# Scaling expert rows at the PSUM eviction and adding them into the output by an accumulating scatter

## The chip, the cores and the metric

The kernel runs on one core of a Trainium2 chip. The metric is the device time of one execution in microseconds (us). Engines are named as in the profile: PE is TensorE, PEld its weight loads, DVE VectorE, ACT ScalarE, POOL GpSimd, SP SyncE.

## What is computed

The program is two decoder layers on x of 8 x 256 tokens (T = 2048) and 512 features: cross-attention, a dense feed-forward layer, cross-attention again, and a mixture of 16 experts. Each is preceded by a layernorm and added to the residual. The change concerns the last of the four:

```
logits = x @ gate_w.T ; p = sigmoid(logits) ; p = p / sum(p)
w, idx = top_k(p, 2) ; w = w / sum(w)
combine = sum(one_hot(idx) * w)                     # (T, 16)
gate, up = split(x @ gate_up_proj[e])               # 512 -> 2*256, for each expert e
y[e] = (silu(gate) * up) @ down_proj[e]             # 256 -> 512
x = x + sum_e combine[:, e] * y[e]
```

## The kernel before

All of it is written by hand: every engine has its own instruction list in each stage, and semaphores order them. The stages before the experts (`load_stage`, `layernorm_stage`, `attention_stage`, `ffn_stage`) keep the residual in SBUF as `k.x_sb`, 16 tiles of 128 tokens by 512 features. The last `layernorm_stage` also stores the normalised rows into `xn_rows` in device memory; SP issues those 16 stores.

`moe_stage` first routes. DVE picks the two best experts of each token, with weights `m1` and `m2`, and ranks the token-expert pairs (4096 of them) by expert. They are packed into 32 tiles of 256 slots (`ROWS`), each tile of one expert; an expert's last tile may be partly empty, and the tiles beyond the last one used are empty altogether. `token_of`, `dest_of` and `expert_of` say for each slot which row to gather, where to put the result, and which expert's weights to load. The index of an empty slot lies out of bounds, so that its descriptor moves nothing.

Then a loop of 16 iterations (`ITER`; the first is written out) does two tiles per iteration, each in two halves of 128 rows: 4 steps per iteration, 64 in all. In step n, PE turns the rows of step n+1 (`turn_x`, L1431), multiplies those of step n by gate and up weights (`gate_up_products`, L1443, 12 matmuls in a hi/lo split of fp32), turns the fused result of step n-1 (`turn_f`, L1453), and multiplies that of step n-2 by the down weights (`down`, L1465, 6 matmuls). ACT makes the hi parts, the silu, and copies the 128x512 result from PSUM to `y_sb[s]` (`copy_y`, L1527). DVE makes the lo parts and the product, and copies the indices for the DMAs (`set_gather`, L1662 and L1663; `set_scatter`, L1669).

POOL issues all indirect DMAs, in this order, once for each half iteration (a tile, b = 0 or 1):

```
gather_weights (L1347)  gather_rows, two DMAs (L1361)  gather_down (L1353)  scatter, scatter (L1369)
```

The gathers are for the next iteration's tile b, the two scatters for the two steps finished last. I call this a POOL group below, its first scatter A and its second B. There are 31 groups with scatters in the loop and one more pair of scatters, without gathers, after it. A gather of rows waits for `gather_set` and `x_turned`. `set_scatter` for a step waits (`y_out`) until the scatter of the same buffer, four steps before, has landed. It stands in the DVE list ahead of the product (`fuse_up`, L1688) of its step.

The scatter writes each pair's unscaled row to `moe_y_rows`, 4096 rows in device memory, two to each token. After the loop SP loads them back in 8 pieces of 1 MB (L1311). DVE multiplies each by `m1` or `m2` and adds it to `k.x_sb` (L1725, 32 instructions), and SP stores the output in 8 pieces (L1314, L1316).

Of the kernel before, what the change touches and what calls it, by code (L numbers as in the profile page):

```python
# [22 lines left out]
P = 128  # L23
# [13 lines left out]
NF = F // P  # L37
E, I = 16, 256
EPS = 1e-5
SM_SCALE = float(HD) ** -0.5  # L40
# [86 lines left out]

def layernorm_stage(k, ahead, rows=None, stats_made=False):

# [5 lines left out]
    with ExitStack() as st:  # L135
# [19 lines left out]
        if rows is not None:  # L155
            rows_out = [k.sem(f"ln_rows_out{i}") for i in range(2)]
            rows_v = rows.rearrange("(t p) d -> p t d", p=P)
# [1032 lines left out]

def moe_stage(k, start, xn_rows, gate_up, down_proj, out):

# [14 lines left out]
    ROUND = 1.5 * 2.0 ** 23  # L1207
    y_rows = nc.dram_tensor("moe_y_rows", (2 * T, D), F32, kind="Internal").ap()

    gu_v = gate_up.rearrange("e (p k) f -> (e p) (k f)", p=P)  # L1210
    dn_v = down_proj.rearrange("e (p k) n -> (e p) (k n)", p=P)
    with ExitStack() as st:
# [3 lines left out]
        def sem(n):  # L1216
            return k.sem(f"moe_{n}")

        def pair(n, shape):
# [19 lines left out]
        before, ones = (sb(n, [P, P], F32R) for n in ("before", "ones"))  # L1239
        before_f, ones_f, after = sb("before_f", [P, P]), sb("ones_f", [P, P]), sb("after", [P, E, E])  # L1240
        cum = sb("cum", [P, NT + 1, E])
# [21 lines left out]
            sem(n) for n in ("gu_made", "silu_done", "fused", "f_turned", "f_hi", "f_split", "y_made", "y_copied"))  # L1263
        gather_set, scatter_set, pairs_in, summed, stored = (
            sem(n) for n in ("gather_set", "scatter_set", "pairs_in", "summed", "stored"))
        pairs_in = [pairs_in, sem("pairs_in1")]
        b_x, b_gu, b_f, b_y = banks[0:2], banks[2:4], banks[4], banks[5:7]
# [30 lines left out]
        @block.sync  # L1298
        def _(sp):
            for s in range(STEPS):  # L1300
                sp.wait_ge(y_out[s], 16 * ITER)
            for b in range(2):
                sp.wait_ge(gu_in[b], 16 * (ITER + 1))
                sp.wait_ge(dn_in[b], 16 * (ITER + 1))
                sp.wait_ge(rows_in[b], 32 * (ITER + 1))
            yv = y_rows.rearrange("(t p k) d -> p t (k d)", p=P, k=2)
            ov = out.rearrange("b (t p) d -> p (b t) d", p=P)
            for n in range(NT // 2):
                if n >= 2:
                    sp.wait_ge(summed, 2 * (n - 1))  # L1310
                sp.dma_start(raw_gu[n % 2][:, :].rearrange("p (t c) -> p t c", t=2), yv[:, 2 * n:2 * (n + 1), :]).then_inc(pairs_in[n % 2], 16)  # L1311
                if n >= 1:
                    sp.wait_ge(summed, 2 * n)
                    sp.dma_start(ov[:, 2 * (n - 1):2 * n, :], k.x_sb[:, 2 * (n - 1):2 * n, :]).then_inc(stored, 16)  # L1314
            sp.wait_ge(summed, NT)
            sp.dma_start(ov[:, NT - 2:NT, :], k.x_sb[:, NT - 2:NT, :]).then_inc(stored, 16)  # L1316
            sp.wait_ge(stored, 16 * NT // 2)

        @block.gpsimd
        def _(pool):  # L1320
# [72 lines left out]
        def _(pe):  # L1393
# [31 lines left out]
            def turn_x(it, s):  # L1425
                if s % HALVES == 0:
                    wait(pe, rows_in[s // HALVES], it, 32, 32)
                wait(pe, x_split, it, STEPS, s - 1)
                by_feature = rows[s][:, :].rearrange("p (q k) -> p k q", k=KD)
# [59 lines left out]
        def _(act):  # L1489
# [65 lines left out]
        def _(dve):  # L1555
# [109 lines left out]
            def set_scatter(it, s):  # L1665
                wait(dve, y_out[s], it, 16, 0)
                reg, add = it
                at = slice(STEPS * add + s, STEPS * add + s + 1) if reg is None else bass.ds(reg * STEPS + (STEPS * add + s), 1)
                v.tensor_copy(scatter_at[s][:, :], dest_of[:, at]).then_inc(scatter_set, 1)  # L1669

            def lo_x(it, s):
# [29 lines left out]
            def body(it):  # L1701
                for s in range(STEPS):
# [13 lines left out]
            lo_f(*step((None, ITER), -1))  # L1716

            for t in range(NT):
                n = t // 2
                if t % 2 == 0:  # L1720
                    dve.wait_ge(pairs_in[n % 2], 16 * (n // 2 + 1))
                for c, weight in enumerate((m1, m2)):
                    y = raw_gu[n % 2][:, D * (2 * (t % 2) + c):D * (2 * (t % 2) + c + 1)]
                    row = k.x_sb[:, t, :]
                    ins = v.scalar_tensor_tensor(row, y, weight[:, t:t + 1], row, ALU.mult, ALU.add)  # L1725
                    ins.then_inc(*((route_chain, 1) if c == 0 else (summed, 1)))
                    if c == 0:
                        done[0] += 1
                        dve.wait_ge(route_chain, done[0])


def decoder_layers(nc, x, ctx_1024, mask, w0, f0, w1, m1, out):
    with ExitStack() as st:
# [10 lines left out]
        k.x_in, k.ctx_stored = [k.sem(f"x_in{i}") for i in range(2)], k.sem("ctx_stored")  # L1744
        k.stats = st.enter_context(nc.sbuf_tensor("ln_stats", [P, NT, 6], F32))
        k.ident_made, k.wait_over = k.sem("ident_made"), k.sem("wait_over")
        k.ln_sems = [k.sem(f"ln_{n}") for n in ("chain", "normed", "act_normed", "turned", "hi_done", "lo_done")]
# [15 lines left out]
        with ExitStack() as ahead:  # L1763
            xn_rows = nc.dram_tensor("xn_rows", (T, D), F32, kind="Internal").ap()
            start = moe_start(k, ahead, m1[0])
            layernorm_stage(k, start, rows=xn_rows, stats_made=True)
            moe_stage(k, start, xn_rows, *m1[1:], out)
# [24 lines left out]
```

## Time and profile before

| | us |
|---|---|
| three timed runs | 2487.07, 2490.06, 2492.52 |
| their median | 2490.06 |
| span of the profiled execution, first to last instruction | 2495.2 |
| PE busy over the span | 2258.1 (90%) |
| DVE busy | 1629.1 (65%) |
| ACT busy | 1238.8 (50%) |
| POOL busy | 719.4 (29%) |
| first row gather of the experts | 2112.96 from the start |
| last PSUM copy of the loop ends | 2446.03 from the start |

The profiled execution is shown by its span; no separate time of it is given, and it is 5.1 us above the median of the timed runs. Positions below are microseconds from the start of the span. DMA instructions on POOL are shown with the time that POOL takes to issue them, not with the time of the transfer. The chain of waits shows a DMA from the start of its issue to its landing.

### The profile page before, as it was taken

To read this page: it belongs to the slowest core of one execution; us is meant where nothing else is said; L and a number is where in the kernel's file an instruction comes from. 1 tells how busy PE (TensorE), PEld (TensorE's weight loads), DVE (VectorE), ACT (ScalarE), POOL (GpSimd) and SP (SyncE) were. 2 spreads that over 40 slices of the span, in tenths; PEclk is the share of its full clock that TensorE was granted. 3 is DMA by queue.
4 is the path that set the end of the run, shared out by engine and by line. 5 is a ranking of instruction groups with operands and counts; after the bars stand their busy time and mean duration, and the time that the engine had idled before them with its cause. 6 is when DMAs were issued, how large, how long until landed. Compare 5 with 4: busy or idle time off the path is not lost. (4 is left out here: it accounts for less than half of the span.)

```text
span 2495.2 us, 40462 instructions
## 1 busy us (share of the span) xinstructions
PE 2258.1 (90%) x12755; PEld 1950.1 (78%) x12755; DVE 1629.1 (65%) x3963; ACT 1238.8 (50%) x3351; POOL 719.4 (29%) x1299
## 2 busy tenths in 40 slices
PE   4999999999995789977999999999999964999992
PEld 4999899999884567766888888888888852878781
DVE  5777777777778952234666666666666676666664
ACT  3545545545543112215666666666666631666661
POOL 1000100100000642223333333433333302666672
PEclk8999999999997999998999999999999986999996
DMA  6111121211101310001111111111211012566405
GB/s 232 60 66 53 59 71 63 71 59 48 65 35 31 94 32 0 0 24 61 43 51 48 70 50 42 67 42 50 72 46 42 35 55 73 205 224 228 156 3 202
DMA packets 77784, 182.74 MB, mean 73 GB/s; under 512 B 13936, under 2 KB 44680, under 8 KB 65952
## 3 DMA queue, kind: packets, MB, share of 16 engines
q1 hardware_dynamic: 57376, 127.46, 14.6%
q0 software_dynamic: 20352, 54.58, 6.2%
q8 instruction: 29, 0.48, 0.1%
q14 instruction: 27, 0.22, 0.0%
HBM read 186.17 MB, written 29.36 MB: 86 GB/s over the span
## 5 line engine op out<-in xcount | busy, mean ns | idle before, releaser
L502 PE MATMUL bank<-l_wkv_hi,l_ctxT 128*128 128x256 f32 (+1 forms) x1024 | 280.3, 346 | 9.4 <-PEq L135 9.0
L791 DVE TENSOR_TENSOR l_v_lo<-bank,l_v_hi 128x128 fp32r<-128x128 f32 (+1 forms) x256 | 91.7, 358 | 223.5 <-ACT l_v_hi L688 222.2
L791 DVE TENSOR_TENSOR l_pT_lo<-bank,l_pT_hi 128x512 fp32r<-128x512 f32 x256 | 175.3, 685 | 81.8 <-ACT l_pT_hi L713 81.8
L502 PE MATMUL bank<-l_wo_hi,l_oT_hi 128*128 128x512 f32 x528 | 216.7, 410 | 3.3 <-DVE l_oT_lo L791 2.8
L707 ACT ACTIVATE l_probs<-l_scored,l_nbias 128x256 f32<-128x256 f32 x256 | 128.2, 502 | 166.8 <-DVE l_nbias L844 163.4
L502 PE MATMUL bank<-xnT_hi,l_wq_hi 128*128 128x512 f32 x512 | 210.1, 410 | 0.0
L502 PEld LDWEIGHTS bank<-l_wkv_hi,l_ctxT 128*128 128x128 f32 x1024 | 184.1, 194 | 30.9 <-issue 9.4
L502 PE MATMUL bank<-l_wo_lo,l_oT_hi 128*128 128x512 f32 x528 | 208.0, 394 | 0.0
L502 PE MATMUL bank<-l_wo_hi,l_oT_lo 128*128 128x512 f32 x528 | 207.0, 392 | 0.0
L502 PE MATMUL bank<-xnT_hi,l_wq_lo 128*128 128x512 f32 x512 | 203.2, 397 | 0.0
L502 PE MATMUL bank<-xnT_lo,l_wq_hi 128*128 128x512 f32 x512 | 202.3, 395 | 0.0
L713 ACT CAST l_pT_hi<-bank 128x512 fp32r<-128x512 f32 x256 | 150.7, 589 | 75.5 <-PE bank L569 75.5
L707 ACT ACTIVATE l_probs<-bank,l_nbias,l_rr 128x256 f32<-128x256 f32 x256 | 142.7, 565 | 86.1 <-DVE l_nbias L834 86.1
L1166 PE MATMUL bank<-xnT_hi,ffn_w 128*128 (+1 forms) x384 | 155.9, 406 | 30.3 <-POOL ffn_w L1060 24.7
L873 DVE TENSOR_TENSOR x_sb<-bank,x_sb 128x512 f32<-128x512 f32 x264 | 175.7, 682 | 2.0 <-PE bank L502 2.0
L502 PE MATMUL bank<-l_wkv_lo,l_ctxT 128*128 128x256 f32 (+1 forms) x512 | 174.9, 342 | 0.0
L859 DVE TENSOR_SCALAR l_probs<-l_probs,l_rden 128x256 f32<-128x256 f32 x512 | 166.6, 368 | 9.0
L502 PE MATMUL bank<-l_pT_hi,l_v_hi 128*128 128x256 f32 x520 | 154.3, 297 | 13.2 <-DVE l_pT_lo L791 13.2
L569 PE MATMUL bank<-ident,l_probs 128*128 128x128 f32 x1024 | 156.1, 275 | 5.8 <-DVE l_probs L859 5.8
L1166 PE MATMUL bank<-xnT_lo,ffn_w 128*128 (+1 forms) x384 | 151.8, 395 | 0.0
L287 POOL TENSOR_TENSOR l_wo_lo<-l_raw_a,l_wo_hi 128x1024 fp32r<-128x1024 f32 x16 | 38.2, 2390 | 393.6 <-ACT l_wo_hi L282 393.6
L502 PE MATMUL bank<-l_kT_hi,l_qT_hi 128*128 128x256 f32 x512 | 147.7, 289 | 3.1 <-DVE l_kT_lo L791 2.2
(237 smaller groups left out, 6431.2 us busy)
## 6 DMA issues: line engine op xcount, KB each, us to landing
l_ctxT<-ctx_split SPq DMA_DIRECT2D x64, 1024.0 KB, 4.8
l_raw_a<-in_L_xattn_Wq SPq DMA_DIRECT2D x16, 512.0 KB, 5.6
l_raw_a<-in_L_xattn_Wo SPq DMA_DIRECT2D x16, 512.0 KB, 5.4
moe_raw_gu<-moe_y_rows SPq DMA_DIRECT2D x8, 1024.0 KB, 6.4
x_sb<-in_x SPq DMA_DIRECT2D x4, 1024.0 KB, 11.3
ctx_split<-ct SPq DMA_DIRECT2D x4, 1024.0 KB, 11.3
xn_rows<-xn SPq DMA_DIRECT2D x16, 256.0 KB, 2.4
out_x<-x_sb SPq DMA_DIRECT2D x8, 512.0 KB, 3.3
```

The lines of the kernel that those rows point to most:

```text
L287: nc.gpsimd.tensor_tensor(w[1], raw, w[0].bitcast(F32), ALU.subtract).then_inc(done, 1)
L502: mm = nc.tensor.matmul(out, a[x], b[y], start=(i == 0), stop=(i == n - 1))
L569: mm = nc.tensor.transpose(b_pt[:, S * s + P * t:S * s + P * (t + 1)], probs[u % 2][:, t, P * s:P * (s + 1)], k.ident[:, :])
L707: ins = nc.scalar.activation(probs[u % 2][:, t, :], src, ACT.Exp, bias=nbias[:, i:i + 1], scale=scale, accum_out=rsum[:, i:i + 1])
L713: nc.scalar.copy(pT[0][:, :, :].rearrange("p s q -> p (s q)"), b_pt[:, :]).then_inc(pT_hi, 1)
L791: nc.vector.tensor_tensor(pair[1], src, pair[0].bitcast(F32), ALU.subtract).then_inc(done, 1)
L859: ins = nc.vector.tensor_scalar(row, row, rden[:, 2 * u + t:2 * u + t + 1], None, ALU.mult)
L873: nc.vector.tensor_tensor(row, b_q[t % 2][:, :], row, ALU.add).then_inc(y_added, 1)
L1166: mm = nc.tensor.matmul(out[f % 2][:, :], w[:, f, first + P * c:first + P * (c + 1)], part[:, c, at], start=(c == 0 and part is k.xnT_hi), ...
```

## The change

Each expert row is now multiplied by its routing weight when it leaves PSUM, and the scatter adds it to a row of the output in device memory.

- The output gets 128 spare rows behind its 2048. The last layernorm stage copies the residual `k.x_sb` into it (4 MB, and 256 KB for the spare rows) after its row stores, on SP's queue.
- `xn_rows` and `rows` have two more columns: `m1` and `m2 - m1` of the token. SP writes them into the 2048 rows by one DMA when DVE has made them (`weights_made`), and POOL waits for it before the first row gather. After the first row gathers POOL waits for the residual copy.
- DVE makes for each slot `second` (1 if it is the token's second choice) and a destination `dest_of`: the token, or a spare row of its own for an empty slot.
- DVE gets one instruction more per step, `weigh`: weight = m1 + second * (m2 - m1), from the gathered row, behind `set_scatter` of that step.
- ACT's `copy_y` becomes an activation with a scale per partition.
- The row gathers wait for `weighed`, two steps back: the gather into tile b of the next iteration waits until both halves of tile b have been weighed.
- Each scatter waits until the one before it has landed (`y_out[s - 1]`), and it adds to its destination.
- The last part, 8 loads, 32 DVE instructions and 8 stores, is gone.

```
@@ layernorm_stage, SP, behind the waits for the row stores
+                sp.dma_start(out_rows[0:T, :].rearrange("(t p) d -> p t d", p=P), k.x_sb[:, :, :]).then_inc(k.out_set, 16)
+                sp.dma_start(out_rows[T:T + P, :], k.x_sb[:, 0, :]).then_inc(k.out_set, 16)
@@ moe_stage, buffers
-        rows = [sb(f"rows{i}", [P, D]) for i in range(STEPS)]
+        rows = [sb(f"rows{i}", [P, D + WEIGHTS]) for i in range(STEPS)]
...
@@ SP
+            sp.wait_ge(weights_made, 1)
+            sp.dma_start(xn_rows.rearrange("(t p) d -> p t d", p=P)[:, :, D:D + WEIGHTS], weights[:, :, :]).then_inc(weights_stored, 16)
...
-            yv = y_rows.rearrange("(t p k) d -> p t (k d)", p=P, k=2)
-            ov = out.rearrange("b (t p) d -> p (b t) d", p=P)
-            for n in range(NT // 2):
...
@@ POOL
             def gather_rows(it, b):
                 wait(pool, gather_set, it, 2, b + 1)
                 wait(pool, x_turned, it, STEPS, HALVES * b - 2)
+                wait(pool, weighed, it, STEPS, HALVES * b - 2)
...
             def scatter(it, s):
                 wait(pool, scatter_set, it, STEPS, s + 1)
                 wait(pool, y_copied, it, STEPS, s + 1)
+                wait(pool, y_out[s - 1], it, 16, 16 if s > 0 else 0)
                 apart(k, pool)
                 at = bass.IndirectOffsetOnAxis(ap=scatter_at[s][:, :], axis=0)
-                gp.indirect_dma_start(y_rows, at, y_sb[s][:, :], None, bounds_check=2 * T - 1, oob_is_err=False).then_inc(y_out[s], 16)
+                gp.indirect_dma_start(out_rows, at, y_sb[s][:, :], None, bounds_check=T + P - 1, oob_is_err=True,
+                                      compute_op=ALU.add).then_inc(y_out[s], 16)
...
+            pool.wait_ge(weights_stored, 16)
             for b in range(2):
                 gather_rows(FIRST, b)
+            pool.wait_ge(k.out_set, 32)
@@ ACT, copy_y
-                nc.scalar.copy(y_sb[s][:, :], b_y[s % 2][:, :]).then_inc(y_copied, 1)
+                wait(act, weighed, it, STEPS, s + 1)
+                nc.scalar.activation(y_sb[s][:, :], b_y[s % 2][:, :], ACT.Copy, scale=weight_of[s][:, :]).then_inc(y_copied, 1)
@@ DVE, routing
+            v.tensor_copy(weights[:, :, 0], m1[:, :])
+            v.tensor_tensor(weights[:, :, 1], m2[:, :], m1[:, :], ALU.subtract).then_inc(weights_made, 1)
...
-            chain(v.tensor_copy(dest_of[:, :], table[:, :]))
+            chain(v.tensor_copy(second[:, :], table[:, :]))
...
+            chain(v.scalar_tensor_tensor(second[:, :], table[:, :], -2.0, second[:, :], ALU.mult, ALU.add))
+            chain(v.tensor_scalar(spare[:, :], part, float(T), None, ALU.add))
+            chain(v.tensor_scalar(dest_of[:, :], table[:, :], spare[:, :], None, ALU.min))
@@ DVE, loop
+            def weigh(it, s):
+                if s % HALVES == 0:
+                    wait(dve, rows_in[s // HALVES], it, 32, 32)
+                wait(dve, y_copied, it, STEPS, s + 1 - STEPS)
...
+                v.scalar_tensor_tensor(weight_of[s][:, :], rows[s][:, D + 1:D + 2], second[:, at], rows[s][:, D:D + 1],
+                                       ALU.mult, ALU.add).then_inc(weighed, 1)
...
                     set_scatter(it, s)
+                    weigh(it, s)
                     fuse_up(it, s)
...
-            for t in range(NT):
-                n = t // 2
-                if t % 2 == 0:
-                    dve.wait_ge(pairs_in[n % 2], 16 * (n // 2 + 1))
...
```

## Rows read from the trace of the kernel before

**Rows 1.** Busy time by stretch: us from the start, length, busy us by engine.

```profile
core 0: us, PE busy (x) PEld busy (x) DVE busy (x) ACT busy (x) POOL busy (x), PEclk, DMA share, GB/s
2130.00:2447.00 317.00, 309.24 (x1497) 254.81 (x1495) 204.16 (x405) 196.70 (x344) 221.46 (x186) 1.00 0.45 157
2447.00:2495.20 48.20, 0.00 (x0) 0.00 (x0) 23.26 (x32) 0.00 (x0) 1.97 (x2) 0.52 0.73 261
```

**Rows 2.** Chain of waits at the end: start us, us, what.

```profile
2445.44 0.59 ACT moe_y_sb L1527
...
2448.57 2.07 DMA moe_y_rows<-moe_y_sb,moe_scatter_at
...
2450.83 4.87 DMA moe_raw_gu<-moe_y_rows
...
2491.26 0.75 DVE x_sb L1725
```

**Rows 3.** Timeline of POOL: start us, us, one group and the next one's start.

```profile
2258.15 1.01 POOL L1361 DMA_INDIRECT moe_rows<-xn_rows,moe_gather_at  x1 [0.31 <-issue]
2259.47 1.57 POOL L1361 DMA_INDIRECT moe_rows<-xn_rows,moe_gather_at  x1 [0.30 <-issue]
2261.34 1.00 POOL L1353 DMA_INDIRECT moe_raw_dn<-in_L_ffn_down_proj,moe_gather_at  x1 [0.30 <-issue]
2262.64 1.03 POOL L1369 DMA_INDIRECT moe_y_rows<-moe_y_sb,moe_scatter_at  x1 [0.30 <-issue]
2263.98 1.67 POOL L1369 DMA_INDIRECT moe_y_rows<-moe_y_sb,moe_scatter_at  x1 [0.30 <-issue]
2267.03 1.05 POOL L1347 DMA_INDIRECT moe_raw_gu<-in_L_ffn_gate_up_proj,moe_gather_at  x1 [1.39 <-DVE moe_gather_at L1663]
```

**Rows 4.** Timeline of DVE: a late scatter, and the indices for that next group.

```profile
2257.58 0.15 DVE L1669 COPY moe_scatter_at<-moe_dest_of 128x1 int32 x1 [1.75 <-DMA moe_y_rows<-moe_y_sb,moe_scatter_at]
...
2265.82 0.15 DVE L1662 COPY moe_gather_at<-moe_expert_of 128x1 int32 x1
2265.89 0.16 DVE L1663 COPY moe_gather_at<-moe_token_of 128x2 int32 x1
```

**Rows 5.** Chain of waits in the loop: scatters that were waited for.

```profile
2252.82 4.63 DMA moe_y_rows<-moe_y_sb,moe_scatter_at
...
2283.41 3.66 DMA moe_y_rows<-moe_y_sb,moe_scatter_at
...
2313.76 4.10 DMA moe_y_rows<-moe_y_sb,moe_scatter_at
...
2324.38 4.70 DMA moe_y_rows<-moe_y_sb,moe_scatter_at
```

**Rows 6.** Chain of waits at the loop's start: a row gather, two gate-up groups.

```profile
2114.48 3.44 DMA moe_rows<-xn_rows,moe_gather_at
...
2120.65 4.95 PE bank L1443 x12
2125.60 0.47 PE bank L1431 x4
2126.07 2.79 PE bank L1443 x12
```

**Rows 7.** Timeline of DVE in the first iteration, indices of step 3.

```profile
2137.22 0.15 DVE L1669 COPY moe_scatter_at<-moe_dest_of 128x1 int32<-128x1 int32 x1
```

**Rows 8.** Timeline of POOL in the first iteration: a row gather, the first scatter.

```profile
2136.38 1.80 POOL L1361 DMA_INDIRECT moe_rows<-xn_rows,moe_gather_at  x1 [0.30 <-issue]
...
2141.09 1.03 POOL L1369 DMA_INDIRECT moe_y_rows<-moe_y_sb,moe_scatter_at  x1 [0.31 <-issue]
```

**Rows 9.** Timeline of DVE in the routing.

```profile
2085.29 0.17 DVE L1605 TENSOR_TENSOR moe_m<-moe_m,moe_ms 128x16 f32<-128x16 f32 x1
...
2111.70 0.20 DVE L1649 CAST moe_token_of<-moe_table 128x68 int32<-128x68 f32 x1
```

**Rows 10.** Timeline of SP: the row stores of the last layernorm.

```profile
2047.88 11.08 SPq L165 DMA_DIRECT2D xn_rows<-xn  x16
```

**Rows 11.** DMA issues: count, KB each, median us from issue to landing.

```profile
l_gain_in<-in_L_xattn_gk SPq DMA_DIRECT2D x1, 0.5 KB, 3.1
```

**Rows 12.** Groups by line from 2020 us: count, busy us and mean ns, idle before.

```profile
L1527 ACT COPY moe_y_sb<-bank 128x512 f32<-128x512 f32 x64 | 37.8, 590 | 45.4 <-PE bank L1465 39.5 <-remote 4.1 <-issue 1.7
...
L223 ACT ACTIVATE xn<-x_sb,ln_shift,ln_rstd 128x512 f32<-128x512 f32 x8 | 6.0, 818 | 17.7 <-DVE ln_shift L194 17.7
```

**Rows 13.** Busy time by stretch: before and among the empty tiles, columns as Rows 1.

```profile
2330.00:2350.00 20.00, 19.70 (x97) 16.62 (x98) 13.95 (x29) 12.35 (x21) 13.07 (x12) 1.00 0.63 217
...
2370.00:2390.00 20.00, 19.37 (x94) 16.10 (x95) 13.41 (x28) 11.45 (x21) 15.41 (x14) 1.00 0.05 9
```

More of the change, by code:

```diff
@@ L38 @@
 E, I = 16, 256
+WEIGHTS = 2
 EPS = 1e-5
@@ L125, in _, with layernorm_stage @@
                                             ct[g][:, 0, c, :].bitcast(F32), ALU.subtract).then_inc(c_lo, 1)
-def layernorm_stage(k, ahead, rows=None, stats_made=False):
+def layernorm_stage(k, ahead, rows=None, stats_made=False, out_rows=None):
     nc, banks = k.nc, k.banks
@@ L156, in layernorm_stage @@
             rows_out = [k.sem(f"ln_rows_out{i}") for i in range(2)]
-            rows_v = rows.rearrange("(t p) d -> p t d", p=P)
+            rows_v = rows.rearrange("(t p) d -> p t d", p=P)[:, :, 0:D]
         @block.sync
@@ L1188, in moe_start, with moe_stage @@
     return a
-def moe_stage(k, start, xn_rows, gate_up, down_proj, out):
+def moe_stage(k, start, xn_rows, gate_up, down_proj, out_rows):
     nc, banks = k.nc, k.banks
@@ L1207, in moe_stage @@
     ROUND = 1.5 * 2.0 ** 23
-    y_rows = nc.dram_tensor("moe_y_rows", (2 * T, D), F32, kind="Internal").ap()
     gu_v = gate_up.rearrange("e (p k) f -> (e p) (k f)", p=P)
@@ L1223, in moe_stage @@
         w_gu, w_dn = ([pair(f"w_{n}{i}", [P, c]) for i in range(2)] for n, c in (("gu", GU), ("dn", DN)))
-        rows = [sb(f"rows{i}", [P, D]) for i in range(STEPS)]
+        rows = [sb(f"rows{i}", [P, D + WEIGHTS]) for i in range(STEPS)]
+        weights = sb("weights", [P, NT, WEIGHTS])
+        weight_of = [sb(f"weight_of{i}", [P, 1]) for i in range(STEPS)]
+        second, spare = sb("second", [P, SLOTS]), sb("spare", [P, 1])
         xT = [[x[:, :, P * i:P * (i + 1)] for x in (k.xnT_hi, k.xnT_lo)] for i in range(2)]
@@ L1239, in moe_stage @@
         before, ones = (sb(n, [P, P], F32R) for n in ("before", "ones"))
-        before_f, ones_f, after = sb("before_f", [P, P]), sb("ones_f", [P, P]), sb("after", [P, E, E])
+        before_f, ones_f = y_sb[0][:, 0:P], y_sb[0][:, P:2 * P]
+        after = y_sb[1][:, 0:E * E].rearrange("p (a b) -> p a b", a=E)
         cum = sb("cum", [P, NT + 1, E])
@@ L1263, in moe_stage @@
             sem(n) for n in ("gu_made", "silu_done", "fused", "f_turned", "f_hi", "f_split", "y_made", "y_copied"))
-        gather_set, scatter_set, pairs_in, summed, stored = (
-            sem(n) for n in ("gather_set", "scatter_set", "pairs_in", "summed", "stored"))
-        pairs_in = [pairs_in, sem("pairs_in1")]
+        gather_set, scatter_set, weighed, weights_made, weights_stored = (
+            sem(n) for n in ("gather_set", "scatter_set", "weighed", "weights_made", "weights_stored"))
         b_x, b_gu, b_f, b_y = banks[0:2], banks[2:4], banks[4], banks[5:7]
@@ L1428, in turn_x @@
                 wait(pe, x_split, it, STEPS, s - 1)
-                by_feature = rows[s][:, :].rearrange("p (q k) -> p k q", k=KD)
+                by_feature = rows[s][:, 0:D].rearrange("p (q k) -> p k q", k=KD)
                 for c in range(KD):
@@ L1669, in set_scatter @@
                 v.tensor_copy(scatter_at[s][:, :], dest_of[:, at]).then_inc(scatter_set, 1)
+            def weigh(it, s):
+                if s % HALVES == 0:
+                    wait(dve, rows_in[s // HALVES], it, 32, 32)
+                wait(dve, y_copied, it, STEPS, s + 1 - STEPS)
+                reg, add = it
+                at = slice(STEPS * add + s, STEPS * add + s + 1) if reg is None else bass.ds(reg * STEPS + (STEPS * add + s), 1)
+                v.scalar_tensor_tensor(weight_of[s][:, :], rows[s][:, D + 1:D + 2], second[:, at], rows[s][:, D:D + 1],
+                                       ALU.mult, ALU.add).then_inc(weighed, 1)
             def lo_x(it, s):
@@ L1716, in _ @@
             lo_f(*step((None, ITER), -1))
-            for t in range(NT):
-                n = t // 2
-                if t % 2 == 0:
-                    dve.wait_ge(pairs_in[n % 2], 16 * (n // 2 + 1))
[L1722 to L1729, printed above, removed]
 def decoder_layers(nc, x, ctx_1024, mask, w0, f0, w1, m1, out):
@@ L1745, in decoder_layers @@
         k.stats = st.enter_context(nc.sbuf_tensor("ln_stats", [P, NT, 6], F32))
+        k.out_set = k.sem("out_set")
         k.ident_made, k.wait_over = k.sem("ident_made"), k.sem("wait_over")
@@ L1763, in decoder_layers @@
         with ExitStack() as ahead:
-            xn_rows = nc.dram_tensor("xn_rows", (T, D), F32, kind="Internal").ap()
+            xn_rows = nc.dram_tensor("xn_rows", (T, D + WEIGHTS), F32, kind="Internal").ap()
             start = moe_start(k, ahead, m1[0])
-            layernorm_stage(k, start, rows=xn_rows, stats_made=True)
+            layernorm_stage(k, start, rows=xn_rows, stats_made=True, out_rows=out)
             moe_stage(k, start, xn_rows, *m1[1:], out)
@@ L1788 @@
         aps.append(nc.dram_tensor(f"in_{name}", a.shape, mybir.dt.from_np(a.dtype), kind="ExternalInput").ap())
-    out = nc.dram_tensor("out_x", (B, S, D), F32, kind="ExternalOutput").ap()
+    out = nc.dram_tensor("out_x", (T + P, D), F32, kind="ExternalOutput").ap()
     decoder_layers(nc, aps[0], aps[1], aps[2], aps[3:7], aps[7:13], aps[13:19], aps[19:22], out)
-    return run(nc, [arrays], core_ids=[0]).results[0]["out_x"]
+    return run(nc, [arrays], core_ids=[0]).results[0]["out_x"][0:T].reshape(B, S, D)
```

9 lines of the change are left out of this document (removed).

## The prediction

> **What bounds the kernel now.** I read the busy time by stretch first. In the expert loop PE is busy for 309 of 317 us at the full granted clock, and POOL for 221; behind the loop PE does nothing for 48 us [rows 1]. The chain of waits says what that end is: the last copy out of PSUM, the last scatter, then loads of the unscaled rows and DVE's additions in turn, to 2495.2 [rows 2]. So two stretches count here: a loop in which PE sets the pace, and a tail of serial transfers. The timelines of POOL and DVE then show how near the loop is to another limit. A POOL group comes each 317/32 = 9.9 us (64 steps, two to a group), and holds six DMA issues of 1.0 to 1.7 us with 0.3 between [rows 3]. DVE already waits now and then for a scatter to land [rows 4], and the chain runs through such landings, 3.66 to 4.70 us after the start of the issue [rows 5]. Nothing yet holds one scatter back for another: B's issue starts 1.3 us after A's [rows 3].
>
> **What goes.** After the last scatter has landed (2448.57 + 2.07 = 2450.6 [rows 2]) 44.6 us are left to 2495.2. The loads, additions and stores in them all go. That is the whole gain, if the last scatter lands when it did.
>
> **The residual copy.** 2176 rows of 2 KB are 4.46 MB. At the 261 GB/s of the tail [rows 1] they take 17 us. SP issues them behind the row stores, about 2059 [rows 10], so they are done near 2078, while DVE routes; POOL asks for them only behind its first row gathers. Price nothing; 17 us if that cover were gone.
>
> **The weights into `xn_rows`.** 2048 pieces of 8 bytes, from about 2085.5, when m2 is ready [rows 9]. POOL wants them at about 2113, just ahead of the gather in [rows 6], so they have 27 us. No row shows so many small pieces. The nearest, 128 of 4 bytes, takes 3.1 us [rows 11]; 16 times that is 50 us. From 3.1 to 50, I take under 27, hidden, since most of 3.1 must be fixed for so few pieces; at worst it costs 22 us once. On SP nothing but final waits stands behind it.
>
> **Routing.** One or two small instructions behind m2 and three behind `token_of`, 0.17 to 0.20 us each [rows 9], on the chain: 1 us with their gaps.
>
> **ACT's scaled eviction.** Between 0.59 us, as now, and 0.82, the activation with scale and bias from SBUF [rows 12]; at worst 64 x 0.23 = 15 us more on an engine busy for 197 of 317 [rows 1]. Nothing.
>
> **The new ring.** This is the step that decides. Three waits close on each other. The row gathers of a POOL group wait for `weigh` of a step whose `set_scatter`, ahead of it on DVE, waits for scatter B of the group before. Behind these gathers in POOL's list stand the down gather, scatter A and scatter B. And B now waits for A to land. Both landings lie in the ring, where before POOL issued on. Its length, from B's landing to the next B's:
>
> - landing to DVE's index copy: 2252.82 + 4.63 = 2257.45 to 2257.58, 0.13 [rows 4, 5]; `weigh` starts 0.07 later, as copies behind each other do [rows 4], and takes about 0.17 [rows 9]: 0.37
> - DVE's result to POOL's issue: 2266.05 to 2267.03, 0.98 [rows 3, 4]
> - two row gathers and the down gather: 2258.15 to 2262.64 is 4.49 [rows 3]; with none longer than 1.0, it is 3.9; I take 4.3, since the queue will be emptier
> - A's landing, La; then 0.98 again for POOL to go on; B's landing, Lb.
>
> So R = 6.63 + La + Lb. The weight gather falls into B's wait. A plain A, behind gathers, has La = 4.3, the mean of the four in [rows 5]. A plain B, alone, lies between 2.07, the last scatter, with hardly a row to write [rows 2], and 3.44, a 256 KB gather behind another [rows 6]; I take 3.1, a full 128 rows with nothing ahead. The add reads the destination first, and no row shows such a transfer: it costs between nothing and another whole landing, 3.44, each time. I take 0.8, of the order of one more pass of the 256 KB (the tail's 261 GB/s at 0.73 busy is 358 GB/s, 0.73 us [rows 1]), nearer the low end as the issue and the completion are not doubled. La = 5.1, Lb = 3.9, R = 15.6 instead of 9.9.
>
> The Trainium skill ("DMA: Bandwidth & Descriptors", section Anatomy of one DMA) prices a DMA issued by GpSimd at 2.0 us and its bytes at 436 GB/s, which makes 2.6 for 256 KB; its 2.0 agrees with the 2.07 above, while the 3.44 is over it. Its "Collectives: The Full Stack" (section The bandwidth ceiling) adds that a reducing DMA costs as much as its two source reads do, not by the add itself, so 3.2; R would be 13.0 and the time 2545.
>
> PE needs 9.9 us a pair of steps and idles for a third. The ring counts from the first scatter: step 3's copy at 2137.22 [rows 7], `weigh` done at 2137.46, + 0.98 + 4.3, + 1 from routing = 2143.7, against 2141.1 now [rows 8]. Thirty rings lead to A of group 31, and one more pair without gathers follows:
>
> 2143.7 + 30 x 15.6 + 2 x (La + Lb = 9.0) + 2 x 0.98 + 0.5 to the end = 2632. Some 8 groups gather nothing (the DMA rate falls from 217 to 9 GB/s [rows 13]), so A waits behind nothing and saves 1.2 each: 2622. That is 127 over the span of 2495.2. The median of the runs is 5.1 below that span, so 2617.
>
> **Other ways.** Each ends on the median's scale.
>
> - The add is free, the queueing is as now: La + Lb = 7.4, R = 14.0, 2566. Chance 0.14.
> - Landings at their bare price: 2.07 and 0.73 for the bytes, 2.8 each, since a serial ring leaves the queue empty. R = 12.2, 2519. The emptier queue speaks for it, [rows 5] against. By the Trainium skill's fit of 2.6 it would be 2506. Chance 0.08.
> - Not slower: the same place, but scatters that land as the nearly empty one, 2.07. With gathers at 3.9, R = 10.4, and the loop costs less than the tail gave: 2460. The point of decision is La + Lb = 4.7 (30 x 6.63 + 32 x 4.7 = 349). 256 KB both ways speak against it. Chance 0.05.
> - The add is dear, a second landing each time: La + Lb = 14.2, R = 20.9, 2786. Chance 0.10.
> - The clock joins in. After PE had waited for its first rows, twelve matmuls took 4.95 us, and 2.79 the next time [rows 6], the 1.2 and the 2.4 GHz level. A ring leaves PE idle for 5 us each time. If all 64 steps went at the low level, 5.0 x 1.77 = 9 us each, PE would set the pace again: 2121 + 64 x 9 + 11 for the last landings is 2708, so 2703. PE's idleness speaks for it; against it, only a part of each ring need be slow, and PE has 5 us to give. Chance 0.08.
>
> **Range and chances.** The forecast, 2570 to 2680, has 0.55. The bounds of the landings, all at their least (3.66 and 2.07, gathers 3.9) and all at their most (8.1 and 6.9, gathers 4.49), make 2499 and 2816. With 0.2 left out the range is 2535 to 2720: it drops the not slower case, the bare price and the dear add. Under 0.2% is what a measurement here can hardly tell from no change: faster 0.04, same 0.01, slower 0.95.
>
> **What would show it.** POOL: the second scatter's issue starts La + 1 (some 6 us) behind the first's, not 1.3; the row gathers start 1.3 us behind a DVE index copy that was released by a scatter; a group each 15.6 us; the issues of the scatters still about 1.0 us. DVE's waits at `set_scatter` grow from some 24 us to over 100. PE's busy share in the loop falls to about two thirds, and no chain piece at the end is a load. The last 44 us are gone. I am wrong if the group's period is still about 10 us, if the scatters' landings differ much from 5 and 4, or if the low clock's matmuls fill the loop.

## The result and the profile after

| | before | after |
|---|---|---|
| median, us (4 runs each) | 2490.91 (2487.07 to 2492.52) | 2677.48 (2675.51 to 2680.88) |
| span of the profiled execution | 2495.2 | 2676.1 |
| PE busy in the expert loop | 309 of 317 | 376 of 520 |
| DVE's waits for a scatter at `set_scatter` | 24.1, 26 times | 209.6, 60 times |

The ratio is 1.075, 95% interval 1.0734 to 1.0764. The kernel is 187 us slower; 2617 was predicted, with 2570 to 2680 for the forecast case and 2535 to 2720 as the range. The measured time lies 2.5 us inside the upper end of the forecast case.

Busy time by stretch, after, with the columns of [rows 1]: the loop from 2130 to 2650, and what is behind it.

```profile
core 0: us, PE busy (x) PEld busy (x) DVE busy (x) ACT busy (x) POOL busy (x), PEclk, DMA share, GB/s
2130.00:2650.00 520.00, 376.04 (x1528) 288.48 (x1528) 220.15 (x479) 209.23 (x351) 242.79 (x188) 0.90 0.49 112
2650.00:2676.00 26.00, 1.50 (x4) 0.67 (x2) 0.00 (x0) 0.69 (x1) 7.02 (x5) 0.57 0.31 40
```

PE has gone from full to 72% busy, with nearly the same number of matmuls. Its busy time is 67 us more. 31 more matmuls fall in the stretch, some 6 us of it, and the rest is that they are slower: the granted clock is 0.90 here where it was 1.00. Of the gate-up matmuls in the stretch (L1442) 113 of 766 take more than 580 ns, against a median of about 395; before (L1443) none of 741 does, and the longest takes 503. The 48 us of loads and additions behind the loop have become 26 us that hold the last scatters. By engine the chain that ended last was led by PE and is now led by DMAs (shares of the whole span). From the page, before:

```profile
PE 11%; DVE 2%; DMA 2%; issue 1%; ACT 0%; POOL 0%; another core or an unknown queue 0%; POOLq 0%; SPq 0%; DVEq 0%; ACTq 0%
```

and after:

```profile
DMA 12%; issue 5%; POOL 2%; DVE 2%; PE 1%; POOLq 1%; ACT 0%; DVEq 0%
```

The ring of the prediction can be read off POOL's timeline (start us, us to issue, idle before and its releaser), one group and the start of the next, after:

```profile
2321.42 1.57 POOL L1365 DMA_INDIRECT out_x<-moe_y_sb,moe_scatter_at  x1 [4.60 <-DMA out_x<-moe_y_sb,moe_scatter_at]
2323.30 1.19 POOL L1341 DMA_INDIRECT moe_raw_gu<-in_L_ffn_gate_up_proj,moe_gather_at  x1 [0.30 <-issue]
2327.97 1.05 POOL L1356 DMA_INDIRECT moe_rows<-xn_rows,moe_gather_at  x1 [3.48 <-issue]
2329.32 1.00 POOL L1356 DMA_INDIRECT moe_rows<-xn_rows,moe_gather_at  x1 [0.30 <-issue]
2330.63 0.99 POOL L1347 DMA_INDIRECT moe_raw_dn<-in_L_ffn_down_proj,moe_gather_at  x1 [0.30 <-issue]
2331.93 1.62 POOL L1365 DMA_INDIRECT out_x<-moe_y_sb,moe_scatter_at  x1 [0.30 <-issue]
2337.97 1.56 POOL L1365 DMA_INDIRECT out_x<-moe_y_sb,moe_scatter_at  x1 [4.42 <-DVE moe_scatter_at L1674]
```

The six DMAs are those of [rows 3], but a group takes 16.55 us and B starts 6.04 us behind A, not 1.3. The releaser named for the row gather is "issue"; what it waited for is in DVE's timeline, after:

```profile
2326.54 0.15 DVE L1674 COPY moe_scatter_at<-moe_dest_of 128x1 int32 x1 [3.00 <-DMA out_x<-moe_y_sb,moe_scatter_at]
2326.74 0.22 DVE L1682 SCALAR_TENSOR_TENSOR moe_weight_of<-moe_rows,moe_second 128x1 f32<-128x1 f32 x1
```

B's landing releases the index copy, `weigh` follows it, and 1.0 us behind `weigh` POOL issues the row gather. The chain of waits gives the landings (start of issue, us to landing), in the same stretch and at the end, after:

```profile
2321.42 4.99 DMA out_x<-moe_y_sb,moe_scatter_at
...
2331.93 5.04 DMA out_x<-moe_y_sb,moe_scatter_at
...
2651.00 4.44 DMA out_x<-moe_y_sb,moe_scatter_at
...
2656.34 4.57 DMA out_x<-moe_y_sb,moe_scatter_at
...
2661.86 4.47 DMA out_x<-moe_y_sb,moe_scatter_at
...
2667.06 1.78 POOLq L1213
```

Where the 180.9 us between the spans lie:

- The first scatter starts at 2151.86, not 2141.09 [rows 8]: +10.8.
- From there to A of the last group with gathers, 30 groups, it is 499.1 us, 16.64 each. Before, it was 10.12 each on the same count (this is 0.2 over the 9.9 that I got by dividing 317 by 32): +195.6.
- From that A to the end it is 25.1 us, and it was 50.6: -25.5.

The sum is 180.9.

### The profile page after: what moved, and what is told of

Read it like the earlier page. It is cut to its first block and busy times, and to the rows that moved or that the text cites. A ratio compares the mean times of both kernels' runs of the same rounds, so it can differ in the third digit from the quotient of the medians.

```text
span 2676.1 us, 40734 instructions
## 1 busy us (share of the span) xinstructions
PE 2319.5 (87%) x12755; PEld 1979.5 (74%) x12755; DVE 1615.0 (60%) x4000; ACT 1247.9 (47%) x3351; POOL 742.0 (28%) x1299
## 5 line engine op out<-in xcount | busy, mean ns | idle before, releaser
L1365 POOL DMA_INDIRECT out_x<-moe_y_sb,moe_scatter_at x64 | 107.3, 1677 | 151.0 <-DVE moe_scatter_at L1674 69.8
## 6 DMA issues: line engine op xcount, KB each, us to landing
out_x<-x_sb SPq DMA_DIRECT2D x1, 4096.0 KB, 12.8
```

Of the source, the lines that this page charges most:

```text
L1365: gp.indirect_dma_start(out_rows, at, y_sb[s][:, :], None, bounds_check=T + P - 1, oob_is_err=True, compute_op=ALU.add).then_inc(y_out[s], 16)
```

## The experiments

All medians in us, each with a ratio to the kernel before on the same chip. Not all kernels ran on the same chip, and the medians of the kernel before lie between 2490.4 and 2492.1, so a difference between two rows can be off by up to 1.7 us. "Per group" is, in the profiled execution, the time from the first scatter to A of the last group with gathers, over 30.

| kernel | median | ratio (95%) | per group |
|---|---|---|---|
| before | 2490.91 | | 10.12 |
| after | 2677.48 | 1.0749 (1.0734 to 1.0764) | 16.64 |
| weigh_early | 2590.55 | 1.0396 (1.0377 to 1.0415) | 13.85 |
| plain_write | 2566.91 | 1.0297 (1.0280 to 1.0314) | 13.15 |
| no_order | 2556.76 | 1.0255 (1.0233 to 1.0276) | 13.24 |
| no_order_weigh_early | 2487.25 | 0.9980 (0.9967 to 0.9993) | 10.92 |
| tile_order | 2499.13 | 1.0038 (1.0024 to 1.0052) | 11.03 |
| tile_order_copy_later | 2494.26 | 1.0014 (1.0005 to 1.0023) | 11.17 |
| tile_order_drop | 2485.21 | 0.9972 (0.9961 to 0.9982) | 10.85 |
| tile_order_drop_plain | 2459.71 | 0.9876 (0.9859 to 0.9892) | 10.03 |
| gathers_between | 2545.36 | 1.0220 (1.0200 to 1.0240) | 12.57 |
| before_wider_rows | 2494.93 | 1.0012 (1.0003 to 1.0021) | 9.98 |

### One wait of the ring moved: weigh_early

`weigh` stood behind `set_scatter` in DVE's list, so the row gathers inherited its wait for scatter B. Here it is made a step ahead, beside the product for the next rows.

```
+            weigh(FIRST, 0)
...
             def body(it):
                 for s in range(STEPS):
...
                     lo_x(*step(it, s + 1))
+                    weigh(*step(it, s + 1))
...
                     set_scatter(it, s)
-                    weigh(it, s)
```

> The weight of a step is made one step ahead, right behind the lo part of its rows, and so no longer behind the wait for a scatter. Adding scatters and the wait of each for the one before stay. Ring theory: the DVE leaves the ring, and only POOL's own list is left in it: landing of A 5.2, 1.0 to go on, issue of B 1.9, weight gather 1.4, three gathers 3.9, so 13.4 us a group instead of 16.6; 31 groups x 3.2 = 99 off, 2578 us. Rival, that the transfers themselves (bandwidth, contention of the adds) set the pace: within 15 us of 2677. Rival, that PE at the low clock sets it: within 15 us of 2677, or slower.

Measured 2590.55, 86.9 us less, and 13 over the number expected. The ring falls open at the gathers: they are now issued straight behind B. POOL's timeline, weigh_early:

```profile
2251.01 1.57 POOL L1365 DMA_INDIRECT out_x<-moe_y_sb,moe_scatter_at  x1 [6.28 <-DVE moe_scatter_at L1674]
2252.89 1.07 POOL L1341 DMA_INDIRECT moe_raw_gu<-in_L_ffn_gate_up_proj,moe_gather_at  x1 [0.31 <-issue]
2254.27 1.05 POOL L1356 DMA_INDIRECT moe_rows<-xn_rows,moe_gather_at  x1 [0.31 <-issue]
...
2258.24 1.62 POOL L1365 DMA_INDIRECT out_x<-moe_y_sb,moe_scatter_at  x1 [0.31 <-issue]
2264.58 1.57 POOL L1365 DMA_INDIRECT out_x<-moe_y_sb,moe_scatter_at  x1 [4.73 <-DMA out_x<-moe_y_sb,moe_scatter_at]
```

A starts 7.2 us behind B here, 10.5 in the group of the kernel after. It does not gain all of B's landing: A now waits for the gathers' issues, and B behind A sometimes waits long, 7.9 us from 2243.11 to 2251.01, with the 1 MB weight gather and the row gathers issued just ahead of A. In the groups 2 to 20, those ahead of the empty tiles, A takes 5.95 us to land on the mean, and 5.3 in the kernel after.

### What the add costs: plain_write

Order, waits and all else as in the kernel after, but the scatter overwrites. The output lacks the sums.

```
-                gp.indirect_dma_start(out_rows, at, y_sb[s][:, :], None, bounds_check=T + P - 1, oob_is_err=True,
-                                      compute_op=ALU.add).then_inc(y_out[s], 16)
+                gp.indirect_dma_start(out_rows, at, y_sb[s][:, :], None, bounds_check=T + P - 1, oob_is_err=True).then_inc(y_out[s], 16)
```

> Only the adding is taken out: the scatters overwrite the output rows instead of adding to them, with every wait in place, so the output lacks the sums. Ring theory with the add dear in itself: landings fall from 5.2 and 4.7 to the plain 4.3 and 3.1 and so does the issue, R from 16.6 to about 14, 2595 us. If the add costs nothing and the length of the landings is due to full 128 rows and the serial order: within 15 us of 2677. If it is the add that costs all: below 2520.

Measured 2566.91: the add costs 110.6 us, a third more than the 82 expected here, and more than twice the 51 that 0.8 us a landing made in the prediction (2617 less 2566). The rows say where. Median time to landing, from the DMA issues, after:

```profile
out_x<-moe_y_sb,moe_scatter_at POOLq DMA_INDIRECT x64, 4.8
```

and in plain_write:

```profile
out_x<-moe_y_sb,moe_scatter_at POOLq DMA_INDIRECT x64, 2.8
```

The issue itself is cheaper too. All scatters of each kernel (issue in ns, least, median and most; first and last start), after:

```profile
L1365 POOL DMA_INDIRECT out_x<-moe_y_sb,moe_scatter_at x64: 1551/1597/2631, 2151.9 to 2667.3; - x64
```

and in plain_write:

```profile
L1365 POOL DMA_INDIRECT out_x<-moe_y_sb,moe_scatter_at x64: 978/1010/1839, 2147.5 to 2553.2; - x64
```

So the add takes 2.0 us more to landing by the medians, and 0.6 of it lies already in the issue. How much of it shows depends on what was issued just ahead. Three landings of a plain write, A, A and B, by the chain of waits, plain_write:

```profile
2213.22 3.48 DMA out_x<-moe_y_sb,moe_scatter_at
...
2251.74 4.93 DMA out_x<-moe_y_sb,moe_scatter_at
...
2257.58 2.76 DMA out_x<-moe_y_sb,moe_scatter_at
```

B, with nothing queued ahead of it, takes 2.74 to 2.78 us as a plain write and 4.4 to 5.6 with the add, mean 4.74: 2.0 more. A, behind three gathers, varies. In the groups 2 to 20 it takes 3.4 to 5.1, mean 4.2, as a plain write and 4.9 to 6.0, mean 5.3, with the add: 1.1 more. Among the empty tiles it is 2.8 against 4.7: 1.9 more.

The Trainium skill ("DMA: Bandwidth & Descriptors", Anatomy of one DMA) gives 2.0 us and the bytes at 436 GB/s, which makes an estimate of 2.6 for 256 KB; the plain 2.76 nearly agrees. Its "Collectives: The Full Stack" (The bandwidth ceiling) lays the lower rate of a reducing step to its two source reads and not to the add. Carried over to this transfer that was my estimate of 3.2; B's mean of 4.74 decides against carrying it over.

### The order taken away: no_order and no_order_weigh_early

The scatters go to rows of their own, 4096 of them, empty slots move nothing, and none waits for another; the add stays. The output holds only the residual. The second kernel has the edit of weigh_early too.

```
-                wait(pool, y_out[s - 1], it, 16, 16 if s > 0 else 0)
...
-                gp.indirect_dma_start(out_rows, at, y_sb[s][:, :], None, bounds_check=T + P - 1, oob_is_err=True,
+                gp.indirect_dma_start(y_rows, at, y_sb[s][:, :], None, bounds_check=2 * T - 1, oob_is_err=False,
                                       compute_op=ALU.add).then_inc(y_out[s], 16)
...
+            chain(v.tensor_copy(dest_of[:, :], table[:, :]))
...
-            chain(v.tensor_scalar(spare[:, :], part, float(T), None, ALU.add))
-            chain(v.tensor_scalar(dest_of[:, :], table[:, :], spare[:, :], None, ALU.min))
```

> The scatters add into a separate array of 4096 rows in which each pair has a row of its own, so that no scatter needs to wait for the one before; the output keeps only the residual, and empty slots move nothing. The wait of the row gathers for the weights stays. Ring theory: one landing leaves the ring: landing of B behind A 5.5, DVE 0.4, POOL 1.0, gathers 3.9, issue of A 1.9, 12.7 us a group, 2677 - 31 x 3.9 = 2556 us. If the order among scatters were all of the cost: about 2470. If it cost nothing: 2677.

> Both edits: unique destinations without order among scatters, and the weights made a step ahead. Output as in the run before, without the sums. Ring theory: no ring is left, POOL issues six DMAs in 9.1 us and PE sets the pace again with 9.9 us a group; the first scatter stands at about 2152, 30 x 9.9 later the last group, and 15 us to the end: about 2465 us, 25 faster than the kernel before. If adding DMAs are slow or crowd the queue by themselves, over 2550.

Measured 2556.76 and 2487.25. The first hit its number, but by luck: a ring through `weigh` is left, and it does not run through B's landing, as the expectation had it. The chain of waits, DVE's timeline and POOL's, no_order:

```profile
2253.24 4.28 DMA moe_y_rows<-moe_y_sb,moe_scatter_at
```

```profile
2257.65 0.15 DVE L1673 COPY moe_scatter_at<-moe_dest_of 128x1 int32 x1 [2.07 <-DMA moe_y_rows<-moe_y_sb,moe_scatter_at]
...
2260.46 0.14 DVE L1673 COPY moe_scatter_at<-moe_dest_of 128x1 int32 x1
```

```profile
2261.74 1.04 POOL L1357 DMA_INDIRECT moe_rows<-xn_rows,moe_gather_at  x1 [2.70 <-PE bank L1430]
```

DVE waits for A, and sets the indices of A's buffer anew 0.12 to 0.13 us behind its landing in each of the 30 groups. The copy for B's buffer comes one DVE step later, 2.8 us here, never with a wait, and at least 0.5 us after B has landed. `weigh` stands behind it, and POOL starts the row gathers 1.0 us behind its end in every group, though the profile names PE as the releaser here. So the ring is A's landing, one step of DVE and the second `weigh`, 1.0 us to POOL and the gathers' issues: 12.45 us here, from A at 2253.24 to A at 2265.69, and 13.24 on the mean. With both waits gone 10.92 a group is left, 0.8 over before, and the time is 22 us over what I expected, as I had priced the add outside the ring at nothing. Its longer issue is 2 x 0.6 = 1.2 us of POOL in each group, and DVE still waits 39.0 us for scatters to land, where it waited 24.1 before.

The waits and the add do not sum up: taking the order away is worth 120.7 us, `weigh` early 86.9, the plain write 110.6, together more than the 196 us that the loop lost. Each alone exposes what it shared with the others, down to the 10 us that the loop needs anyway.

### A version that keeps the sums: tile_order and tile_order_copy_later

Only rows that may be the same row need an order. The pairs of one expert's tile have 256 different tokens, so A and B of a tile never meet. With `weigh` early, A waits for both scatters of the tile before, and B for nothing. Each half has its own 128 spare rows. The second kernel also lets SP issue the residual copy at the start of the expert stage instead of the end of the layernorm.

```
                 wait(pool, y_copied, it, STEPS, s + 1)
-                wait(pool, y_out[s - 1], it, 16, 16 if s > 0 else 0)
+                if s % HALVES == 0:
+                    for other in (s - 2, s - 1):
+                        wait(pool, y_out[other], it, 16, 16 if s > 0 else 0)
...
+            chain(v.tensor_scalar(spare[:, :], part, float(T + P), None, ALU.add))
+            chain(v.tensor_scalar(dest_of[:, 1::2], table[:, 1::2], spare[:, :], None, ALU.min))
...
@@ second kernel: from the end of layernorm_stage to SP's start in moe_stage
+            sp.dma_start(out_rows[0:T, :].rearrange("(t p) d -> p t d", p=P), k.x_sb[:, :, :]).then_inc(k.out_set, 16)
+            sp.dma_start(out_rows[T:, :].rearrange("(t p) d -> p t d", p=P), k.x_sb[:, 0:2, :]).then_inc(k.out_set, 16)
             sp.wait_ge(weights_made, 1)
```

> All sums are computed. The two scatters of a POOL group hold rows of one expert, so no token is in both; they are issued one behind the other, each half with its own 128 spare rows, and only the next group's first scatter waits for them. The weights are made a step ahead. Ring theory: B's landing is 4.8 + 1.0 behind its issue, and POOL's next four gathers and B's own issue take 7.2, so the wait is hidden; like no_order_weigh_early, 2487 us, within 10. Rival, that the gain of no_order_weigh_early came from the empty slots that moved nothing: at least 30 more than 2487. Rival, that any order among scatters costs a landing a group: 2487 + 31 x 4 = 2610.

> As tile_order, and SP issues the residual copy at the start of the expert stage and not at the end of the layernorm stage. If the stage's end waits for SP to finish issuing (0.4 + 4.1 us): PE's first instruction of the expert stage 4.5 us earlier, and the time 4 to 5 below tile_order. If the copy's 4.5 MB crowd the first weight gathers: no gain or a loss.

Measured 2499.13 and 2494.26. The loss is gone but for 7 and 2 us. The first is 12 us over the 2487 expected, where I had allowed 10; the empty slots, below, are most of that. The place of the copy is worth 4.9 us by the medians. The runs of the two kernels overlap (2496.6 to 2504.8 and 2492.9 to 2501.8), but their intervals of the ratio do not, and SP's and PE's timelines show a cause of that size. SP's in tile_order:

```profile
2060.49 0.39 SPq L169 DMA_DIRECT2D out_x<-x_sb  x1
2060.93 4.06 SPq L170 DMA_DIRECT2D out_x<-x_sb  x1
```

The first matmuls of the expert stage, PE's timeline, tile_order:

```profile
2065.43 0.58 PE L1397 MATMUL bank<-ident,moe_gw 16*128 16x16 f32 x4 [6.85 <-PEq L136]
```

and tile_order_copy_later, where the same two issues start at 2061.45 and PE does not wait for them:

```profile
2061.49 0.58 PE L1397 MATMUL bank<-ident,moe_gw 16*128 16x16 f32 x4 [3.66 <-PEq L136]
```

Counted from the first row store's issue (2045.13 and 2045.88), PE starts the stage 4.7 us earlier with the copy moved. The copy's landing was hidden as I had said. Its issue was not: SP is held for 4.1 us by the second of the two DMAs, and PE starts right behind it.

### Empty slots that move nothing: tile_order_drop and tile_order_drop_plain

Empty slots get an index out of bounds again, as before the change, where tile_order adds each of them to a spare row. The second kernel overwrites instead of adding, and lacks the sums.

```
-            chain(v.tensor_scalar(dest_of[:, :], table[:, :], spare[:, :], None, ALU.min))
+            chain(v.tensor_copy(dest_of[:, :], table[:, :]))
...
-                gp.indirect_dma_start(out_rows, at, y_sb[s][:, :], None, bounds_check=T + 2 * P - 1, oob_is_err=True,
+                gp.indirect_dma_start(out_rows, at, y_sb[s][:, :], None, bounds_check=T + P - 1, oob_is_err=False,
                                       compute_op=ALU.add).then_inc(y_out[s], 16)
@@ second kernel
-                gp.indirect_dma_start(out_rows, at, y_sb[s][:, :], None, bounds_check=T + P - 1, oob_is_err=False,
-                                      compute_op=ALU.add).then_inc(y_out[s], 16)
+                gp.indirect_dma_start(out_rows, at, y_sb[s][:, :], None, bounds_check=T + P - 1, oob_is_err=False).then_inc(y_out[s], 16)
```

> As tile_order_copy_later, but the index of an empty slot lies out of bounds, so that an empty slot moves nothing, and there is no use for the spare rows. If the transfers of empty slots cost time only where nothing waits: within 5 us of tile_order_copy_later, of it 2 us at the last landing. If they crowd the queue: 10 or more faster.

> As tile_order_drop, but the scatters overwrite instead of adding, so the output lacks the sums. In tile_order_drop no ring is left, and yet a loaded group takes 10.7 us where the kernel before takes 10.0. If the add still costs there by its longer issue on POOL (1.6 instead of 1.0, twice a group) and its double traffic (DMA busy 0.75 against 0.64): a loaded group falls to 10.0 to 10.2, and the time by 10 to 16 to 2470 or so. If the rest is due to the new waits and weights: within 3 us of 2485.

Measured 2485.21, 9.1 us under tile_order_copy_later and 0.28% under the kernel before: the fastest of the versions that compute the whole result, and the only one of these with its interval below 1. The 9.1 us lie between the two numbers expected; the time per group makes 9.6 of them, 6.0 in the last ten groups, where most of the empty tiles are. Without the add it is 2459.71, another 25.5 us, or 24 by the ratios, since the chips differ; I had expected 10 to 16. The add's price where hardly a scatter waits for another is thus some 24 us. Where it lies is seen in the busy time between 2160 and 2300, tile_order_drop:

```profile
2160.00:2300.00 140.00, 128.68 (x601) 103.75 (x601) 84.27 (x188) 79.74 (x137) 100.07 (x77) 0.98 0.75 205
```

and tile_order_drop_plain:

```profile
2160.00:2300.00 140.00, 136.06 (x664) 113.21 (x663) 92.63 (x205) 90.15 (x152) 94.78 (x84) 1.00 0.64 227
```

In the same 140 us PE does 601 matmuls with the add and 664 without, POOL is busier for fewer DMAs, and the DMA engines are busier while they move less. DVE's waits for a scatter's landing also fall, from 39.0 us to 21.2. How the 24 us divide between POOL's issues, the DMA engines and these waits was not separated.

### Where in the queue A stands: gathers_between

All scatters in order again, `weigh` early, but POOL issues A ahead of the row and down gathers and B behind them, so that A lands while POOL issues.

```
                     gather_weights(after_it, b)
+                    done = b == 1 or it is not FIRST
+                    if done:
+                        scatter(before_it if b == 0 else it, HALVES * (1 - b))
                     gather_rows(after_it, b)
                     gather_down(after_it, b)
-                    if b == 1 or it is not FIRST:
-                        for h in range(HALVES):
-                            scatter(before_it if b == 0 else it, HALVES * (1 - b) + h)
+                    if done:
+                        scatter(before_it if b == 0 else it, HALVES * (1 - b) + 1)
```

> As weigh_early, with the full order among scatters, but POOL issues scatter A ahead of the row and down gathers and B behind them, so that A's landing has other issues to hide behind. All sums are computed. If a landing takes 4.8 wherever it stands: two landings of 4.8 + 1.0 a group, 11.6 us instead of 13.9, 2590 - 31 x 2.3 = 2520 us. If a scatter lands only behind what was queued ahead of it, A behind the weight gather (1 MB) and B behind the row and down gathers (1 MB), each 1 to 2 us later: 13 to 14 us a group, 2560 to 2590.

Measured 2545.36, between the two numbers expected. POOL's timeline, A and B twice, gathers_between:

```profile
2243.37 1.60 POOL L1365 DMA_INDIRECT out_x<-moe_y_sb,moe_scatter_at  x1 [2.94 <-ACT moe_y_sb L1529]
...
2249.52 1.61 POOL L1365 DMA_INDIRECT out_x<-moe_y_sb,moe_scatter_at  x1 [0.58 <-issue]
...
2255.66 1.60 POOL L1365 DMA_INDIRECT out_x<-moe_y_sb,moe_scatter_at  x1 [2.73 <-DMA out_x<-moe_y_sb,moe_scatter_at]
...
2263.23 2.64 POOL L1365 DMA_INDIRECT out_x<-moe_y_sb,moe_scatter_at  x1 [2.01 <-DMA out_x<-moe_y_sb,moe_scatter_at]
```

A's landing is mostly covered by the three issues behind it (6.15 us from A to B in the first pair; in the second B still waits 2.0 us for it), but B's is not. The order of the queue is worth 45 us at the same number of waits; tile_order, where B waits for nothing and A's wait is mostly over by its turn, is worth 91 over weigh_early.

### The front alone: before_wider_rows

The kernel before, with rows of 514 columns in `xn_rows` and `rows`, and one DMA of 2048 pieces of 8 bytes into them.

```
-            xn_rows = nc.dram_tensor("xn_rows", (T, D), F32, kind="Internal").ap()
+            xn_rows = nc.dram_tensor("xn_rows", (T, D + 2), F32, kind="Internal").ap()
...
-        rows = [sb(f"rows{i}", [P, D]) for i in range(STEPS)]
+        rows = [sb(f"rows{i}", [P, D + 2]) for i in range(STEPS)]
...
+            sp.dma_start(xn_rows.rearrange("(t p) d -> p t d", p=P)[:, :, D:D + 2], ...).then_inc(gw_in, 16)
```

> The kernel before, with two more columns in the rows in device memory and in SBUF, filled by one DMA of 2048 pieces of 8 bytes (with numbers that nothing uses). Tells what row length and small pieces cost. If the row stores' 4.0 us to land instead of 2.4 come from the row length: the first instruction of the expert stage about 2 us later and the time 2 to 4 above the kernel before. If they came from the residual copy behind them: no change.

Measured 2494.93, 2.8 us over the kernel before on that chip. DMA issues, before_wider_rows:

```profile
xn_rows<-xn SPq DMA_DIRECT2D x16, 256.0 KB, 4.2
xn_rows<-moe_counts_i SPq DMA_DIRECT2D x1, 16.0 KB, 3.9
```

The row stores take 4.2 us each to land instead of 2.4, with nothing changed for them but that the rows no longer lie end to end. PE starts the stage 16.1 us behind the first row store's issue, 14.8 before. The many small pieces, which I had bounded by 50 us, land in 3.9.

## Why the prediction was right, and by how much its terms were off

The step that was to decide did: a ring through both landings, on which PE waits. Of the rivals, the free add and the bare landings fell with the rows above, though 2.8 was the right price for a plain B (2.76). The not slower case needed La + Lb = 4.7, and in the groups of the kernel after it is 9.0 to 11.6; the dear add needed 14.2. The clock rival named a real effect, 0.90 granted, but PE is idle for 144 us of the loop's 520, and moving one small DVE instruction took 87 us off: PE did not set the pace.

On the scale of the span, the terms of the prediction make 2622.6 and 2676.1 was measured, 53.5 more. The terms:

- **Thirty rings: +40.7.** They were to take 30 x 15.6 less 8 x 1.2 for the empty tiles, 458.4, and took 499.1. The means of the thirty: landing to the row gather 1.52 (1.35 forecast), gathers 4.27 (4.3), La 5.12 (4.78 with the empty tiles), on to B 0.99 (0.98), Lb 4.74 (3.9). The mis-sized term is the add, most of all in Lb, where I took 0.8 and a scatter with nothing ahead of it pays 2.0. Two errors offset each other in part: my plain B was 3.1, and it is 2.76. La came nearly right, as the plain 4.3 was near the measured 4.2 and the add costs less behind gathers, 1.1.
- **The empty tiles saved nothing**: the first twenty rings took 16.55 each, the last ten 16.81. A's landing did fall, from 5.3 to 4.7 on the mean. The plain A falls by 1.35, as foreseen, but the add's price rises there from 1.1 to 1.9. And in most of these groups one of the three issues took 2.0 us where it had taken 1.0. POOL's timeline, after, from B to the next B among the empty tiles, 16.74 us:

```profile
2624.13 1.57 POOL L1365 DMA_INDIRECT out_x<-moe_y_sb,moe_scatter_at  x1 [3.98 <-DMA out_x<-moe_y_sb,moe_scatter_at]
...
2631.68 2.04 POOL L1356 DMA_INDIRECT moe_rows<-xn_rows,moe_gather_at  x1 [0.30 <-issue]
...
2640.87 1.56 POOL L1365 DMA_INDIRECT out_x<-moe_y_sb,moe_scatter_at  x1 [3.92 <-DVE moe_scatter_at L1674]
```

- **The first scatter: +8.2** (2151.86 for 2143.7). PE's first instruction of the stage is 6.9 us later than before, at 2069.59. 1.1 of it was there already when the first row store was issued. The wider rows make 1.3, by the same stretch in before_wider_rows, and the copy's two issues 4.5. The step "residual copy: nothing" failed: it looked at the landing (12.8 us, hidden) and not at the issues, which hold SP at the end of a stage. Behind PE's start the first scatter comes 3.9 us later than before, where I had 2.6; with `weigh` early it is 0.7, so `weigh`'s place makes 3.2 of it. I can't say what in that is longer than forecast. SP's and PE's timelines, after:

```profile
2065.07 4.08 SPq L170 DMA_DIRECT2D out_x<-x_sb  x1
```

```profile
2069.59 0.57 PE L1395 MATMUL bank<-ident,moe_gw 16*128 16x16 f32 x4 [8.36 <-PEq L136]
```

- **The end: +4.6** (25.1 for 20.5). The last scatters were sized well: the last one lands at 2671.9, 20.9 us behind the last group's A, for 20.0. Then POOL's drain at the end of the block goes on to 2675.9. The line of it, after (ns, start):

```profile
L1213 POOLq DRAIN  x1: 8849/8849/8849, 2667.1 to 2667.1; - x1
```

Before, the same drain of 10.98 us began at 2446.6, and the loads and additions of the tail covered it. In plain_write it ends 6.3 us beyond the last landing and 8.1 behind the last issue, here 4.1 and 7.1; what it waits for stays open.

- **ACT's eviction** takes 0.69 us, within 0.59 to 0.82. Its price of nothing was not tested by itself; ACT is busy for 209 of the loop's 520 us. The weights' DMA landed in 4.0 us of the 27 there were. That the scatter's issue would stay at 1.0 us was wrong: it is 1.60. In the ring this lies within the landing; outside it, it is part of the 24 us of tile_order_drop_plain.

## What to carry to other kernels

A wait that orders two DMAs puts a whole landing, here 4.4 to 6.0 us, and 1 us from its semaphore to the next issue, on POOL's list, and everything queued behind it there pays; so order only those transfers that can touch the same rows, and put work between the two that must be ordered. Before a value's maker is placed behind another in an engine's list, ask what the other waits for: one 0.2 us `weigh` behind an index copy closed a second ring, worth 87 us. An adding scatter costs more than a plain one: 2.0 us more to landing with nothing ahead of it, 1.1 behind gathers, and 0.6 more on POOL for each 128 rows. Even where hardly a scatter waits, that took some 24 of the 44.6 us that the tail gave back, and the best version gains only 7.

## What the runs showed of the hardware that was not expected

- An indirect DMA that adds takes POOL 1.60 us to issue where the plain one takes 1.01, and one of 128 rows of 2 KB with nothing queued ahead lands in 4.4 to 5.6 us (mean 4.74), where the plain one takes 2.76.
- POOL's drain behind a block with indirect DMAs lasted 8.85 us from its start, 4.1 us beyond the last landing.
- A 256 KB store into rows 2056 bytes apart lands in 3.7 to 4.2 us (medians of the runs), into rows of 2048 bytes that lie end to end in 2.4.
- The issue of the 256 KB copy behind the 4 MB copy held SP for 4.1 to 4.3 us.
- 2048 pieces of 8 bytes landed in 3.6 to 4.1 us, hardly more than the 3.1 of 128 pieces of 4 bytes [rows 11].
